# Where a value step of cross-attention leaves its first group of heads

## The reference

```python
# x (4, 2048, 512), ctx (4, 77, 512), mask (4, 2048, 77), 16 heads of 32
qs = heads(x @ wq); ks = heads(ctx @ wk); vs = heads(ctx @ wv)
scores = where(mask, -inf, qs @ ks.T / sqrt(32))
attn = softmax(scores) @ vs
out = merge(attn) @ wo + x
y = (out - mean(out)) / sqrt(var(out) + 1e-5) * gamma + beta      # over the 512 columns
```

## Time and profile before

| | |
|---|---|
| median of 3 runs | 617.94 us (617.9 to 618.48) |
| profiled execution | span 616.2 us; no time of its own is recorded beside it |
| TensorE busy | 599.4 us, 97% |
| DVE / ScalarE / GpSimd busy | 84% / 82% / 80% |
| granted clock of TensorE | 0.999 of full speed (mean) |

### The profile page before, as it was taken

One profiled execution on the slowest core, in us unless ns is written; L12 is line 12 of the kernel. 1 busy time (PEld: TensorE's weight loads), 2 busy tenths in 40 slices (PEclk: granted clock), 3 DMA queues, 4 the chain that ended last, 5 costly groups with the idle time before them and its releaser, 6 DMA issues.

```text
span 616.2 us, 12956 instructions
## 1 busy us (share of the span) xinstructions
PE 599.4 (97%) x3856; PEld 476.5 (77%) x3856; DVE 520.4 (84%) x1060; ACT 506.6 (82%) x1558; POOL 491.3 (80%) x639
## 2 busy tenths in 40 slices
PE   9998999999999999999999999999999999998995
PEld 7876687877878787787878788787878878786763
DVE  6677798898888889888888988898888889888888
ACT  6788888988888898888889888888988888886851
POOL 4587458897979889797979979797997979687784
PEclk9999999999999999999999999999999999999999
DMA  8621475463655546355654645555463555643103
GB/s 281 198 67 52 131 192 178 124 187 111 170 146 160 171 141 180 106 171 143 164 165 120 180 129 168 149 160 159 123 176 116 163 151 138 206 106 102 53 36 119
DMA packets 62165, 89.22 MB, mean 145 GB/s; under 512 B 20368, under 2 KB 20880, under 8 KB 62096
## 3 DMA queue, kind: packets, MB, share of 16 engines
q1 hardware_dynamic: 62096, 88.39, 50.1%
HBM read 39.53 MB, written 16.78 MB: 91 GB/s over the span
## 4 chain that ended last, share of the span: by engine, by line
PE 82%; DVE 6%; POOL 4%; ACT 4%; issue 2%; POOLq 0%; DVEq 0%; ACTq 0%
PE bank L433 27%; PE bank L529 24%; PE bank L479 7%; PE bank L469 6%; PE bank L463 5%; PE bank L502 4%; PE bank L483 2%; PE bank L507 2%; ACT pr L639 2%; PE bank L409 1%; DVE al L811 1%; PE bank L460 1%; ACT ah L607 1%; POOL pn L977 1%; DVE pr L789 1%
## 5 line engine op out<-in xcount | busy, mean ns | idle before, releaser
L639 ACT ACTIVATE pr<-pr,nm 128x77 f32<-128x77 f32 x1024 | 270.0, 349 | 39.5 <-DVE nm L795 35.9
L977 POOL TENSOR_TENSOR pn<-pr,rec 128x512 f32<-128x512 f32 x128 | 134.8, 1053 | 77.7 <-DVE rec L804 76.1
L789 DVE SCALAR_TENSOR_TENSOR pr<-msk,bank 128x308 f32<-128x308 uint8 x256 | 109.3, 468 | 33.6 <-PE bank L469 28.6
L802 DVE TENSOR_REDUCE sm<-pr 128x8 f32<-128x616 f32 x128 | 100.6, 786 | 9.7 <-ACT pr L639 9.3
L795 DVE TENSOR_REDUCE nm<-pr 128x8 f32<-128x616 f32 x128 | 101.7, 795 | 4.4
L529 PE MATMUL bank<-woh,ah 128*128 128x512 f32 x256 | 103.8, 405 | 1.4 <-DVE al L811 1.3
L433 PE MATMUL bank<-xh,wqh 128*128 128x512 f32 x256 | 103.2, 403 | 0.0
L607 ACT ACTIVATE ptr<-bank 128x512 f32<-128x512 f32 (+1 forms) x256 | 95.7, 428 | 8.8 <-PE bank L479 8.7
L529 PE MATMUL bank<-woh,al 128*128 128x512 f32 x256 | 101.3, 396 | 0.0
L529 PE MATMUL bank<-wol,ah 128*128 128x512 f32 x256 | 101.1, 395 | 0.0
L433 PE MATMUL bank<-xh,wql 128*128 128x512 f32 x256 | 100.3, 392 | 0.0
(11 more groups left out here) (94 smaller groups left out, 1020.5 us busy)
## 6 DMA issues: line engine op xcount, KB each, us to landing
qd<-qn SPq DMA_DIRECT2D x224, 128.0 KB, 2.6
xraw<-xT SPq DMA_DIRECT2D x58, 256.0 KB, 3.4
xres<-x SPq DMA_DIRECT2D x58, 256.0 KB, 2.8
out<-y SPq DMA_DIRECT2D x56, 256.0 KB, 2.0
ptr<-xT SPq DMA_DIRECT2D x6, 256.0 KB, 9.0
zt<-x SPq DMA_DIRECT2D x6, 256.0 KB, 4.1
out<-zt SPq DMA_DIRECT2D x6, 256.0 KB, 2.0
wk_sb<-wk SPq DMA_DIRECT2D x4, 256.0 KB, 4.8
```

What stands on the lines that cost most here:

```text
L639: last = nc.scalar.activation(s, s, ACT.Exp, bias=nm[:, t % 2, h:h + 1], scale=1.0)
L789: nc.vector.scalar_tensor_tensor(out=pr[:, 4 * g:4 * g + 4, :], in0=msk[:, m % MR, t % 4, :].unsqueeze(1).broadcast_to([P, 4, LK]), scalar ...
L802: nc.vector.tensor_reduce(sm[:, t % 2, hs], pr[:, hs, :], AX.X, ALU.add).then_inc(v_sum, 1)
L977: nc.gpsimd.tensor_tensor(pn[:, half, 0:4, :].rearrange("p s (e k) -> p (s e) k", e=2), pr[:, hs, 0:KM], rec[:, t % 2, hs].unsqueeze(2).br ...
```

## The change

Part (1, 0) of the value steps e = 0 to 13 goes to a bank of `MB`, and such a step takes two neighbouring places of the rotation, ("v", e, 0) and ("v", e, 1). Both are asked for before the matmuls of half 1 (the old place was asked for at the head of the step). The fifth transpose behind it has no wait for `v_al`. The steps of the written-out end keep the old bank `PTB[1]` and one place.

```diff
-            misc += [("v", VALUES[t])] if t in VALUES else []
+            misc += [("v", VALUES[t], j) for j in range(2)] if t in VALUES else []
...
-        misc += [("o", T - 10), ("o", T - 9), ("v", E - 3), ("o", T - 8), ("o", T - 7), ("o", T - 6), ("v", E - 2),
-                 ("o", T - 5), ("o", T - 4), ("o", T - 3), ("v", E - 1)]
+        misc += [("o", T - 10), ("o", T - 9), ("v", E - 3, 1), ("o", T - 8), ("o", T - 7), ("o", T - 6),
+                 ("v", E - 2, 1), ("o", T - 5), ("o", T - 4), ("o", T - 3), ("v", E - 1, 1)]
...
-            kind, i = misc[n]
+            kind, i, *part = misc[n]
...
-                pe.wait_ge(v_al, 4 * i + 2)
+                pe.wait_ge(v_al, 4 * i + part[0] + 1)
...
-            return {(1, 0): PTB[1], (1, 1): misc_bank(("v", e)), (0, 0): AVB[0], (0, 1): AVB[1]}[part]
+            if part == (1, 0):
+                return misc_bank(("v", e, 0)) if e < E - 3 else PTB[1]
+            return {(1, 1): misc_bank(("v", e, 1)), (0, 0): AVB[0], (0, 1): AVB[1]}[part]
...
             def weigh_v(e):
                 t, n = STEPS[e]
                 b, cols = t // TB, columns(e)
-                misc_free(pe, ("v", e))
...
                 for half in range(2):
                     pe.wait_ge(a_pt, 2 * (t + n - 1) + half + 1)
+                    if half == 1:
+                        if e < E - 3:
+                            misc_free(pe, ("v", e, 0))
+                        misc_free(pe, ("v", e, 1))
...
-                    transpose_p(t - 1, 0, after=VALUES[t])
+                    transpose_p(t - 1, 0)
```

## The result

The changed kernel took 624.09 us (median of 4 runs, 621.55 to 625.5) against 618.1 us: ratio 1.009, interval 1.0072 to 1.0109. It is slower, as forecast, but by 6.0 us and not by 1.9, outside the range. So there are two questions: what the steady 3 us are made of, and what the first four runs had beside them.

What follows compares the result with a forecast made beforehand. TensorE's gapless matmul stream was taken to bound the kernel; +2.12 us at the first step and -0.26 over 13 regular steps gave +1.86, so 619.8 us from a median of 617.94, range 618.7 to 621.0.

Steps and rivals of the forecast that it cites:

- the first step: At e = 0 project_q(9) newly waits for the first low part, released at 70.39: +2.12 us, not given back.
- the moved wait: In 13 regular steps the low-part wait moves from the fifth transpose to the query projection, saving 0.07 us a step.
- rival (a): Full 0.28 us idle time at the low-part wait recovered in each of 13 steps, 3.64 us: 616.4 us; 5%.
- the wait in the middle of the weighing: Half 1 of regular weighings waits for the output projection's residual: +0.05 us a step, between nothing and 0.14.
- the wait at half 1 of e = 0: Wait for low_q(8) in the first weighing: at most 0.08 us, ahead of the new idle time, so costing nothing.
- the step that gave the fall of the clock 2%: TensorE's clock falling to 1.2 GHz behind the new idle time at e = 0: 2.8 us more, 622.6 us; 2%.
- rival (e): Clock falls to 1.2 GHz for the 12 matmuls of the projection at e = 0: 2.8 us more, 622.6 us; 2%.
- Loads come relatively earlier: After the first step's delay, no DMA is issued, removed or moved past a queue, so loads come relatively earlier; no size.

Runs made afterwards that it cites:

- a1_again: The changed kernel once more, same file with no edit, against the kernel before: 621.22 us, ratio 1.005.
- e2_first: Only the first value step e = 0 changed, e = 1 to 13 as in the kernel before: 620.39 us, ratio 1.0037.
- e6_swap: The changed kernel with the two places of a step exchanged, so the projection waits for the second low part: 631.44 us, ratio 1.0203 against the kernel before.
- e7_slice: The kernel before, with one projection slice issued ahead of the fifth transpose's wait in the 13 regular steps: 614.68 us, ratio 0.9941.
- e4_wait: The kernel before, with only a wait for the residual added at half 1 of weighings e = 1 to 13: 620.15 us, ratio 1.0032.
- f2_idle: The kernel before, with a wait for the third low part ahead of project_q(9): 626.02 us, ratio 1.0126.
- e5_order: The changed kernel with transposes (4, 0) issued ahead of project_q(9) at t = 5: 619.63 us, ratio 1.0019 against the kernel before.
- e1_rest: The change without its first step, only e = 1 to 13 changed, against the kernel before: 619.02 us, ratio 1.0013.
- e8_first: The kernel before, with one projection slice ahead of the fifth transpose in 13 regular steps and three at t = 5, after the four transposes: 614.4 us, ratio 0.9939.
- e3b_fill: The changed kernel with 8 unread matmuls ahead of project_q(9), run again for a profile: 621.3 us, ratio 1.0052 against the kernel before.
- f1_idle: The kernel before, with a wait for the second low part ahead of project_q(9): 621.07 us, ratio 1.0054.

## Why the prediction was right in direction and wrong in size

**Right: the first step.** "+2.12 us", "so it stays", the release near 70.4 and nothing given back: 2.16 us in a1_again, 2.19 in e2_first, 2.15 with the idle time filled. This is the larger part of the steady loss, and it comes from a wait of the first step alone.

**Right: the moved wait.** It moved past one transpose, and the saving was 0.07 us a step. e6_swap shows that the new place binds in every step. e7_slice shows what rival (a) priced at 3.64 us: with work ahead of the release the idle time is worth 0.25 us a step by the profile and 3.6 us in all by the medians. The change moved the wait and did not fill it.

**Mis-sized: the wait in the middle of the weighing.** This is the term that failed in the steady kernel. I took +0.05 us; it costs 0.14 (e4_wait 0.13 to 0.15), the upper bound. The reckoning was 0.75 from the residual's start to the release and 1.02 from there to L507; measured are 322.50 - 321.71 = 0.79 and 323.56 - 322.50 = 1.06, and the residual starts 0.17 instead of 0.16 us after the weighing. Three errors of hundredths, all one way, made -0.02 a step into +0.08, 13 times: 1.3 us. The same reckoning had put the wait at half 1 of e = 0 at 0.08 us at most; in the changed kernel it is 0.17 (65.45 - 64.32 between its two groups of weight loads, 65.36 - 64.40 before), but it lies ahead of the long idle time and costs nothing, as said.

**Wrong: the step that gave the fall of the clock 2%.** This is the step that failed in the profiled execution of the first four. "The granted clock stayed at the upper of its levels through an idle time of 1.34 us ...; the new idle time is longer" named the mechanism and then took it as all but excluded, from one trace in which the clock happened to stay up: behind the same wait it fell in the profile of e2_first. In the profiled execution it was there: 4.21 us for the first to last matmul of `project_q(9)` instead of 2.65, 1.6 us. The Trainium skill's warning of idle gaps ("TensorE: Matmul & The Clock Gate", "Why this matters for your kernels") agrees in kind with f2_idle, where it fell, by the mean clock, in all of four executions after 5.54 us. The price of rival (e), 2.8 us, was too high: eight of the twelve matmuls were spaced at the lower level, and each cost 0.20 us more (0.43 - 0.23) and not 0.23.

**Not foreseen: the copy of `kh`.** "Loads come relatively earlier" was wrong at one place. TensorE and the DMA queue of SP in the changed kernel's profile, at the turn from batch 0 to 1:

```profile
166.27 0.41 PE L465 MATMUL bank<-kh,ql 128*128 128x308 f32 x1 [0.72 <-DMA kh<-khc]
...
158.20 4.16 SPq L323 DMA_DIRECT2D qd<-qn  x4
162.40 2.59 SPq L294 DMA_DIRECT2D kh<-khc  x4
```

Issuing four copies of `qd` took 4.16 us instead of 2.53 before, and the copies of `kh` queued behind came late. The single issues show why; the third row is of the kernel before:

```profile
158.71 1.59 SPq L323 DMA_DIRECT2D qd<-qn  x1
160.98 1.37 SPq L323 DMA_DIRECT2D qd<-qn  x1
...
157.60 1.45 SPq L292 DMA_DIRECT2D kh<-khc  x1
```

Most issues there take about 0.6 us. The kernel before has one long one at this turn, among the copies of `kh`; the changed kernel has two, both ahead of them. The step from e = 2 to 3 took 36.87 us, 36.05 in a1_again, 36.00 before. TensorE's weight load waited for `kh` there for 0.96 us in the changed kernel and 1.26 in e6_swap (two long issues too), for 0.65 in e2_first and 0.43 in e5_order, for 0.23 to 0.34 in e1_rest, e4_wait, e8_first and f2_idle, and not at all before and in a1_again, e3b_fill, e7_slice and f1_idle.

**The account.** Span of the changed kernel's profile over that of before, 5.7 us: 2.2 for the wait at e = 0, 1.6 for the clock, 0.8 at the turn of the batch, 1.0 for the regular steps; 5.6 together. a1_again has the first and the last of these alone: 3.2 us by the distances, 2.9 by the medians. So the forecast of +1.9 missed the steady loss by 1.0 us (1.3 by the distances), in the regular steps, and the first four runs by 4. The direction was forecast for the right reason; the first measurement lay as high as 6.0 us because of things that vary between executions, two of which the profiled one shows: the clock and the copy of `kh`.

**What stays open.** Whether the idle time of 1.7 us itself decides on the fall of the clock, or what goes on beside it: the changed kernel's first step had the clock down in one profile and up in the other. Only the profiled one of the first four runs can be taken apart: why another took 624.47 us at a mean clock of 0.997, and a third only 621.55 at 0.995, isn't known. It isn't recorded on which chip the first four ran, so a difference between chips isn't excluded as a part of the 3 us between the two medians. And whether a late first step makes the wait for `kh` likelier: of the eight profiles with a late first step five waited, of the five others three, and more briefly.

## What to carry to other kernels

When a bank is moved into a rotation, write down for every use behind it which earlier use it now waits for, in the first iteration too: the steady steps lost 0.08 us each, the first lost 2.2 us, because there the order on TensorE was another. A wait on the bounding engine is worth its idle time only if independent work is put ahead of it: here one slice of a projection between two transposes brought 3.6 us, where moving the result to another bank brought a loss. And price a new idle time of TensorE twice, with the clock up and with the work behind it at the lower clock.

## What the runs showed of the hardware

**The clock behind short idle times.** The granted clock of TensorE fell in the middle of a kernel that is otherwise 97% busy, and not every time. At the first step, after idle times of 1.12 us (e5_order) and 1.67 us (a1_again, e2_first) it was up; after 1.68 us (the changed kernel), 2.26 (e6_swap), 2.44 (f1_idle) and 5.54 us (f2_idle) it was down in the profiles. By mean clock and time it was up in one other execution of e6_swap and in three of f1_idle. At the wait near the end, 1.34 to 1.38 us in every profile here, it stayed up in all of them but e2_first, where it fell after 1.35 us. At the lower level a 512-column matmul followed the last after 0.43 us instead of 0.23. Two profiles of the same file, the changed kernel's and that of a1_again, differ by 1.6 us at the first step for this reason alone.

**A wait inside a group of small-tile matmuls.** The wait at half 1 cost 0.14 us a step. Before, the weight loads of half 1 came in two groups, 0.46 and 0.89 us after the first load of the weighing (316.97 and 317.40, that one at 316.51); with the wait all 16 come together at 0.96 (322.50, after 321.54). The last loads are thus only 0.07 us later, the closing group 0.14. That the loss comes from the early loads, which had been running ahead of the matmuls, is read from these rows and was not tested by itself.

**The issue of a DMA.** On SyncE's queue at the turn of the batch most issues took about 0.6 us. One took 1.45 us in the kernel before, two took 1.59 and 1.37 in the changed kernel, 1.50 and 1.79 in e6_swap. What makes one long isn't known.
